# Reciprocal roots of the first graph stage once a group of eight row sets on VectorE, and GpSimd's fill behind every eight sends

## The reference

```
x = x + gnn0(layernorm(x))     # spectral graph layer: U^T, W1, relu, W2, U
x = x + ffn0(layernorm(x))     # 8 experts, best 2 of each token, silu
x = x + gnn1(layernorm(x))     # graph convolution with two batch norms
x = x + ffn1(layernorm(x))     # 8 experts, best 2, and one shared, gelu
layernorm(x) = (x - mean) / sqrt(var + 1e-5)
```

## Time and profile before

| quantity | value |
|---|---|
| median of 3 runs | 1314.97 us |
| the profiled execution | 1320.74 us, span 1318.9 us |
| busy: PE, DVE, ACT, POOL | 84%, 68%, 45%, 37% of the span |
| first stage with its sends | about 289 to 418 us |
| experts of layer 0 | from 422.5 us |
| second graph stage with its sends | about 842 to 1004 us |
| indirect sends of rows, both layers (L1052) | 128, mean 996 ns |

### The profile page before, as it was taken

The page is one execution under the profiler, slowest core; times in us unless marked ns, Lnnn a source line. Parts: engine busy times, 40 slices in busy tenths (PEclk is TensorE's granted clock), DMA queues, the critical chain, the costliest instruction groups (busy, mean ns, idle before and its releaser), DMA issues.

```text
span 1318.9 us, 25232 instructions
## 1 busy us (share of the span) xinstructions
PE 1105.5 (84%) x7060; PEld 924.3 (70%) x7060; DVE 896.8 (68%) x3848; ACT 594.3 (45%) x1786; POOL 488.8 (37%) x539
## 2 busy tenths in 40 slices
PE   3556555658874999999999999798889999999995
PEld 3555544646652888978889754376667998899994
DVE  5777689865775666756667597688753667556683
ACT  2556844507771222212222267466534444444452
POOL 2200000002665444434444461005763555445551
PEclk9999999959996999999999999899889999999998
DMA  9999996000223444323332250001224444233317
GB/s 190 404 428 428 429 426 262 1 0 26 86 87 120 128 123 126 101 72 103 94 91 70 84 207 1 16 5 66 90 85 123 143 144 125 68 114 109 110 55 198
DMA packets 78875, 182.67 MB, mean 138 GB/s; under 512 B 11752, under 2 KB 51699, under 8 KB 75408
## 3 DMA queue, kind: packets, MB, share of 16 engines
q0 software_dynamic: 20544, 112.80, 21.5%
q1 hardware_dynamic: 58192, 68.27, 19.2%
HBM read 65.10 MB, written 119.08 MB: 140 GB/s over the span
## 4 chain that ended last, share of the span: by engine, by line
PE 63%; DVE 25%; issue 5%; ACT 3%; DMA 1%; SPq 1%; another core or an unknown queue 0%; POOL 0%; DVEq 0%; POOLq 0%; ACTq 0%
PE bank L1707 18%; PE bank L1693 17%; PE bank L1696 7%; PE bank L199 4%; PE bank L1933 3%; PE bank L1926 3%; PE bank L1679 2%; PE bank L1860 2%; DVE work L337 2%; DVE u L334 2%; PE bank L900 1%; DVE bnh L1761 1%; PE bank L1441 1%; DVE u L184 1%; DVE u L175 1%
## 5 line engine op out<-in xcount | busy, mean ns | idle before, releaser
L1693 PE MATMUL bank<-work,wide 128*128 128x256 f32 (+3 forms) x994 | 215.4, 330 | 3.3 <-issue 1.9
L1707 PE MATMUL bank<-wide,work 128*128 128x128 f32 x1512 | 216.5, 278 | 0.6 <-DVE work L1623 0.4
L1707 PEld LDWEIGHTS bank<-wide,work 128*128 128x128 f32 x1512 | 198.1, 191 | 9.5 <-DVE work L1623 3.4
L1052 POOL DMA_INDIRECT rows<-tokens,slot x128 | 127.4, 996 | 202.9 <-issue 142.1
L1651 ACT ACTIVATE work<-bank 128x256 f32<-128x256 f32 (+1 forms) x216 | 82.8, 383 | 261.2 <-PE bank L1696 232.8
L1693 PEld LDWEIGHTS bank<-work,wide 128*128 128x128 f32 (+1 forms) x994 | 154.1, 186 | 16.2 <-issue 4.1
L1538 POOL DMA_INDIRECT rows<-wide x100 | 104.7, 1047 | 121.3 <-DVE wide L1575 101.2
L199 PE MATMUL bank<-u 63*64 63x2 f32 (+61 forms) x496 | 73.7, 255 | 66.3 <-DVE u L184 65.3
L1623 DVE TENSOR_TENSOR work<-work,bank 128x256 f32<-128x256 f32 (+1 forms) x216 | 88.3, 417 | 41.1 <-ACT work L1651 36.2
L1559 DVE COPY wide<-wreg 128x1066 f32 (+1 forms) x142 | 100.4, 707 | 21.6 <-issue 18.0
L199 PEld LDWEIGHTS bank<-u 63*64 63x64 f32 (+61 forms) x496 | 64.4, 217 | 71.8 <-DVE u L184 70.5
(11 more groups left out here) (449 smaller groups left out, 2405.0 us busy)
## 6 DMA issues: line engine op xcount, KB each, us to landing
rows<-wide POOLq DMA_DIRECT2D x20, 3432.0 KB, 109.7
wide<-rows SPq DMA_DIRECT2D x100, 260.0 KB
wide<-rows SPq DMA_DIRECT2D x88, 130.0 KB
wreg<-in_w SPq DMA_DIRECT2D x1, 4264.0 KB, 38.8
wreg<-in_w SPq DMA_DIRECT2D x1, 4112.0 KB, 14.1
tokens<-in_x SPq DMA_DIRECT2D x2, 2048.0 KB, 20.2
tokens<-in_xt SPq DMA_DIRECT2D x1, 4096.0 KB, 41.7
tokens<-plane SPq DMA_DIRECT2D x16, 256.0 KB, 5.2
```

The source lines that it names most:

```text
L1052: return self.nc.gpsimd.indirect_dma_start(out=xs, out_offset=bass.IndirectOffsetOnAxis(ap=self.t["slot"][:, q:q + 1], axis=0), in_=self.t ...
L1693: ins = T.matmul(ps[c][0:n, to], w[:, a:a + n], x[:, to], start=True, stop=True)
L1707: ins = T.matmul(ps[4 + j % 2][:, h * P:(h + 1) * P], t["hh"][c][0:n, h * P:(h + 1) * P], w[0:n, at + c * P:at + (c + 1) * P], start=(c == ...
```

## The change

Three edits. `TOGETHER` is 8 instead of 4, so that each fill stands behind eight sends. In `gnn0` the epsilon, ACT's square root, the reciprocal and the offset of each tile are gone; in their place stands `roots(g)` at the end of every even step from step 2, which runs the eleven operations of `inverse_root` and one offset operation for a whole group of eight sets on DVE. And ACT writes the normalised rows of a group's two tiles at the head and at the end of its odd step.

```diff
-TOGETHER = 4
+TOGETHER = 8
 def gnn0_act(nc, act, S, t, ps, route):
+    def normalised(i):
+        act.wait_ge(S("a0_norm"), i // GT + 1)
+        for q in range(PAIRS):
+            at = (i % GT) * PAIRS + q
+            ins = A.activation(t["pay"][:, i * PAIRS + q, 0:P], t["X"][:, i * PAIRS + q, :], ACT.Identity,
+                               bias=t["off"][:, at:at + 1], scale=t["rs"][:, at:at + 1])
+        ins.then_inc(S("a0_xh2"), 1)
-        if 0 <= s - 2 < TILES:
-            i = s - 2
-            act.wait_ge(S("a0_norm"), i + 1)
...
-            ins.then_inc(S("a0_xh2"), 1)
+        if due(s, GT + 1):
+            normalised(s - 3)
...
-        if 0 <= s - 1 < TILES:
-            act.wait_ge(S("a0_var"), s)
-            A.activation(t["sd"][:, 1, :], t["sd"][:, 0, :], ACT.Sqrt).then_inc(S("a0_root"), 1)
+        if due(s, GT + 1):
+            normalised(s - 2)
 def gnn0_dve(nc, dve, own, S, t, ps, route):
-        def variance():
...
-            V.tensor_scalar(t["sd"][:, 0, :], t["mv"][:, :, 1], EPS, None, ALU.add).then_inc(S("a0_var"), 1)
+        def roots(g):
+            dve.wait_ge(S("a0_moments"), GQ * (g + 1))
+            if g:
+                dve.wait_ge(S("a0_xh2"), GT * g)
+            for k in range(ROOT_OPS):
+                inverse_root(V, dve, pair, S("a0_inv"), g, k)
+            dve.wait_ge(S("a0_inv"), (g + 1) * ROOT_OPS)
+            V.scalar_tensor_tensor(out=t["off"], in0=pair["mv"][:, :, 0], scalar=-1.0, in1=t["rs"], op0=ALU.mult,
+                                   op1=ALU.mult).then_inc(S("a0_norm"), 1)
+            dve.wait_ge(S("a0_norm"), g + 1)
-        if old:
-            dve.wait_ge(S("a0_root"), T + 1)
-            if T >= 2:
-                dve.wait_ge(S("a0_xh2"), T - 1)
-            own.chain(V.reciprocal(t["rs"][:, half], t["sd"][:, 1, :]))
-            V.scalar_tensor_tensor(out=t["off"][:, half], in0=t["mv"][:, :, 0], scalar=-1.0, in1=t["rs"][:, half],
-                                   op0=ALU.mult, op1=ALU.mult).then_inc(S("a0_norm"), 1)
-            dve.wait_ge(S("a0_norm"), T + 1)
...
-            variance()
+            for g in due(s, GT):
+                roots(g)
```

More of the change, by code:

```diff
@@ L1341, in gnn0_act @@
             A.copy(t["gm"][i % 2], ps[2][:, :]).then_inc(S("a0_gm"), 1)
-        if 0 <= s - 1 < TILES:
-            act.wait_ge(S("a0_var"), s)
-            A.activation(t["sd"][:, 1, :], t["sd"][:, 0, :], ACT.Sqrt).then_inc(S("a0_root"), 1)
+        if due(s, GT + 1):
+            normalised(s - 2)
 def gnn0_dve(nc, dve, own, S, t, ps, route):
-    V, X = nc.vector, t["X"]
+    V, X, pair = nc.vector, t["X"], t["pair"]
     for s in range(A0_STEPS):
-        T, T1 = s - 2, s - 1
-        old, new = 0 <= T < TILES, 0 <= T1 < TILES
+        T1 = s - 1
+        new = 0 <= T1 < TILES
         xt = X[:, T1 * PAIRS:(T1 + 1) * PAIRS, :] if new else None
@@ L1364, in stats @@
                 dve.wait_ge(S("a0_xadd"), T1 + 1)
+                if T1:
+                    dve.wait_ge(S("a0_moments"), T1 * PAIRS)
             V.bn_stats(t["bn"][:, q, :], xt[:, q, :]).then_inc(S("a0_stats"), 1)
@@ L1370, in moments @@
             dve.wait_ge(S("a0_stats"), T1 * PAIRS + q + 1)
-            V.bn_aggr(t["mv"][:, q, :], t["bn"][:, q, :]).then_inc(S("a0_moments"), 1)
-        def variance():
-            if not new:
-                return
-            dve.wait_ge(S("a0_moments"), (T1 + 1) * PAIRS)
-            V.tensor_scalar(t["sd"][:, 0, :], t["mv"][:, :, 1], EPS, None, ALU.add).then_inc(S("a0_var"), 1)
+            V.bn_aggr(pair["mv"][:, (T1 % GT) * PAIRS + q, :], t["bn"][:, q, :]).then_inc(S("a0_moments"), 1)
+        def roots(g):
[8 more added lines that the diff above has]
+            dve.wait_ge(S("a0_norm"), g + 1)
         def by_choice(k):
@@ L1385, in by_choice @@
                 moments(k - 6)
-            elif k == 10:
-                variance()
-        if old:
-            half = slice((T % 2) * PAIRS, (T % 2 + 1) * PAIRS)
-            dve.wait_ge(S("a0_root"), T + 1)
-            if T >= 2:
-                dve.wait_ge(S("a0_xh2"), T - 1)
-            own.chain(V.reciprocal(t["rs"][:, half], t["sd"][:, 1, :]))
-            V.scalar_tensor_tensor(out=t["off"][:, half], in0=t["mv"][:, :, 0], scalar=-1.0, in1=t["rs"][:, half],
-                                   op0=ALU.mult, op1=ALU.mult).then_inc(S("a0_norm"), 1)
-            dve.wait_ge(S("a0_norm"), T + 1)
         if due(s, GT + 1):
@@ L2194, in build @@
         t["sdi"] = t["sd"][:, :, :].bitcast(I32)
-        t["rs"], t["off"] = sb("rs", [P, 2 * PAIRS])[:, :], sb("off", [P, 2 * PAIRS])[:, :]
+        pair = dict(mv=sb("pair_mv", [P, GQ, 2]), sd=sb("pair_sd", [P, 3, GQ]))
+        pair["sdi"] = pair["sd"][:, :, :].bitcast(I32)
+        t["pair"], t["rs"], t["off"] = pair, pair["sd"][:, 1, :], sb("off", [P, GQ])[:, :]
         nm = sb("norm", [P, 2, 2, PAIRS])
```

## The result

The changed kernel takes 1302.99 us, the median of four runs (1302.79 to 1303.84), against 1315.08 of the kernel before (four runs, 1312.74 to 1316.63). The ratio is 0.9911, 95% interval 0.9894 to 0.9928: faster by 12.1 us. The forecast was 7.6 us, and the time lies 0.5 us under the lower end of the range. The profiled execution took 1302.85 us, its span is 1301.0.

A forecast was written before the change was run, and what follows sets the result against it. The start of layer 0's experts was taken as set by POOL's last send, fed by DVE's loop. Loop 5.5, first steps 1.2 and fill 0.9 made 7.6 us, from 1314.97 to 1307.4 us; range 1303.5 to 1312.5.

The forecast's parts named there:

- The loop: First stage's loop on DVE: period falls from 12.71 to 11.8 us (11.2 to 12.5), six periods giving 5.5 us.
- PE's count: First stage's loop: DVE's wait for PE's count of a group comes out, 0.5 us, between 0 and 1.30.
- The first steps: Layer 0, ahead of the first send: roots of four tiles go, two chains come in; 1.2 us gain, between 0 and 3.0.
- The fill in layer 0: POOL in the first stage: one fill less from group 6 to group 7 counts in full, 0.9 us.
- The sum at the last send: POOL's last send in layer 0 comes 7.6 us earlier: 5.5 + 1.2 + 0.9.
- The products, the load of the first rows and the experts then shift as a block: Layer 0 after POOL's last send: all 7.6 us pass on to the experts.
- 8 x 0.94 = 7.5 us less of POOL is worth 0 here: Layer 1: halving the fills gains nothing, as POOL ends 9 us before PE starts the experts.
- up to 7.5: Layer 1: what fewer fills would be worth in us if the 9 us of cover were gone.
- Locks: Rival: the twelve DVE operations each lose 0.25 us beside POOL's sends; period 14.8, time 1328 us; chance 0.05.
- the upper end that the prediction gave these two: DVE's chain: two tensor_scalar operations held beside POOL each lose 0 to 0.25 us, 0.5 at most; 0.1 taken.
- The second stage moves: Rival: DVE's operations meet other sends there; one more wait for a count gives 1310.8 us, one less 1304.0; chance 0.13.
- The sign by which I would be wrong: Experts of layer 1 starting at another distance from those of layer 0 than 581.45 us.

The follow-up runs named there:

- the fourth: The changed kernel with the fill behind every four sends in layer 1 alone, layer 0 as changed: 1306.85 us, ratio 0.9940.
- the 1310.5: A profiled execution of the kernel before, unchanged, run again for a second trace: 1310.5 us; the median of its eight runs was 1315.21.
- the 1320.74: The first profiled execution of the kernel before, unchanged, whose trace the prediction read: 1320.74 us.

## Why the prediction was wrong

**The loop: right.** Period 11.76 against 11.8; chain 2.45 against 2.36, 0.20 an operation; PE's count 0.54 a group against 0.5. Six periods gave 5.7 us, 5.5 forecast.

**The first steps: right, somewhat low.** The profiled pair shows 0.8. The six profiles without the new roots start their first send at 319.8 us in the mean (318.7 to 320.3), the eight with them at 318.0 (317.2 to 318.7): 1.8, where I had 1.2 between 0 and 3.0.

**The fill in layer 0: right.** From group 6 to group 7 11.51 against 12.27, 0.8 (forecast 0.9), and the kernel with roots alone shows the pace of 12.2 that the prediction gave for the fills as before (12.1). The sum at the last send was 7.2 in the pair, 7.6 forecast; between the means of the four profiles of before and of the four with both edits in layer 0 and six warming products (the changed kernel, the fourth, the fourth with two products more, and the one without layer 1's fills) it is 7.9.

**"The products, the load of the first rows and the experts then shift as a block": failed.** The load came 7.1 us earlier (SP's first at 412.74, before 419.88), the experts 5.9; between the same means the last send is 7.9 earlier and the experts are 7.1. I had carried over 6.93 us for the warming products, a duration taken while the clock was rising. They begin when POOL's small fill is there, and PE's wait for it had shrunk from 3.79 to 0.28 us, where I had 1.0, as PE's limits came 3.7 us earlier and not 5. So, by the estimates above, about 5.9 us of the products ran at 0.50 in place of 3.1. The price was 1.3 us in the pair, 0.8 between the means; four products instead of six gave about as much back.

**"8 x 0.94 = 7.5 us less of POOL is worth 0 here": failed, and this is what put the time out of the range.** It was 3.8 us on top of the rest; with these the 1302.99 would be 1306.8, inside the range. Two things were wrong in the reading of the earlier trace rows. The cover was counted from POOL's last fill, 994.92, to the experts, 1003.93. But the experts need the rows, and these came 5.56 us after the last send had started in the 1310.5: 993.49 + 5.56 = 999.05, against 1003.21 for PE's last product. The cover was about 4.2 us, not 9. And that execution was late in just this stage, 161.89 us against 154.35 to 157.01 in the three others: PE came late and hid POOL. Of this lateness the waits for the counts, among them, are 2.5 us (13.0, against 10.4 to 10.5 in the three others); the rest is not traced to one place. In the other executions of before the two paths arrive within 2 us of each other, and whoever is late decides; in the 1310.5 PE waits 1.89 us, and the clock is at 0.50 in the 5 us behind it. The prediction did say what the cover's loss would cost, "up to 7.5", and gave it no chance.

The sums. The chances add up to 0.78 for faster and 0.17 for same by the terms given, where the prediction has 0.77 and 0.18. In the earlier trace rows the L1174 of 948.84 begins 0.07 us ahead of the send, so it is not inside it; the operations behind it are.

The rivals. Locks did not come in the changed kernel. Grouped by line, the chain's operations in its first stage (times, busy us, mean ns):

```profile
L1174 DVE TENSOR_TENSOR pair_sd<-pair_sd 128x8 f32<-128x8 f32 x24 | 4.4, 183 | 0.8
L1176 DVE TENSOR_TENSOR pair_sd<-pair_sd 128x8 f32<-128x8 f32 x24 | 4.0, 166 | 0.8
L1178 DVE SCALAR_TENSOR_TENSOR pair_sd<-pair_sd 128x8 f32<-128x8 f32 x24 | 4.0, 166 | 0.8
...
L1172 DVE TENSOR_SCALAR pair_sd<-pair_sd 128x8 int32<-128x8 int32 x8 | 1.4, 172 | 0.3
L1170 DVE TENSOR_SCALAR pair_sd<-pair_mv 128x8 f32<-128x8 f32 x8 | 1.4, 171 | 0.3
```

The ten with two inputs run for the most part beside sends and take 166 ns each, but for the first L1174 of six chains, up to 235 ns, where a send starts 0.03 or 0.04 us behind it. By the rule of the Trainium skill, "SBUF — State Buffer", section "Who interferes with whom", the operations with two SBUF inputs would contend with a GpSimd instruction that reads SBUF; so far as a send is such a read, which no run here shows, this trace disagrees. The two scalar operations, L1170 and L1172, have no send beside them at all here: POOL is waiting for the gates that DVE made just ahead of the chain. With roots alone POOL has no such wait, and there they are held (shortest, median and longest in ns; then one chain and POOL beside it):

```profile
L1170 DVE TENSOR_SCALAR pair_sd<-pair_mv x8: 171/468/518, 300.3 to 389.2; 128x8 f32<-128x8 f32 x8
```

```profile
340.13 0.47 DVE L1170 TENSOR_SCALAR pair_sd<-pair_mv 128x8 f32<-128x8 f32 x1
340.63 0.44 DVE L1172 TENSOR_SCALAR pair_sd<-pair_sd 128x8 int32<-128x8 int32 x1
```

```profile
339.62 0.98 POOL L1052 DMA_INDIRECT rows<-tokens,slot  x1 [0.30 <-issue]
340.59 0.45 POOL L1047 MEMSET idle<- 128x400 f32 x1
```

L1170 ends with the send and L1172 with the fill, and the chain takes 2.95 us, 0.5 more, the upper end that the prediction gave these two. So this lock exists, and the change escaped it because both edits came together. "The second stage moves" was the nearest to what happened, as it forecast one wait less and 1304.0, but its mechanism, DVE's operations meeting other sends, was not the one. The sign by which I would be wrong, another distance than 581.45 us between the layers' experts, came: 572.73. But it was a poor sign, as the unchanged kernel shows 572.76, 577.85 and 576.12 in its three other traces.

## What to carry to other kernels

A cover that is read in one execution is worth no more than that execution: before an engine's work is costed at nothing, follow what it releases through the transfer to the instruction that needs it, and ask whether the covering engine was late there by a wait that need not come again. A distance read in one execution cannot be the sign of a change before it is known how far it moves without one. Two edits that each relieve one of two nearly equal paces should be costed together, since either alone may give half or nothing. And where TensorE waits at a seam, the price of the wait is the wait and the low clock behind it; a few products in the wait can be worth more than the wait itself, and too many become the path.

## What the runs showed of the hardware

- The clock behind a wait. With PE's idle time ahead of layer 1's experts at 0.72 (nine profiles), 0.97 and 0.47 us the clock stays at 1.00; at 1.89, 2.34 and 2.43 us it is 0.50 over the first 5 us of the experts. The eight products of L1693 take 1.97 us in the one case and 3.75 in the other. One profile of the first kind is as long as those of the second, the 1320.74, with its 314.97 us: its clock is 1.00, and PE is busy 38.21 of the 40 us from 1083.93 on, 39.64 at the same place of the changed kernel. Why is open.
- Layer 0's six warming products took 6.86 to 7.56 us in the seven profiles where PE had waited 1.7 to 3.8 us for POOL ahead of them, and 7.72 to 8.33 in the four where it had waited 0.2 to 0.3.
- A tensor_scalar operation of 128x8 on DVE beside GpSimd: in the kernel with roots alone L1170 took 468 ns in the median and L1172 430, against 171 and 172 with nothing on GpSimd beside them; the one shown ended with a send, the other with a fill. Operations with two inputs of the same size took 166 ns in the median there, sends beside them or not.
- Rows sent by indirect DMA were back in SBUF for PE 5.5 to 6.0 us after the last send had started on POOL, where PE waited for them (409.55 to 415.06, 988.72 to 994.28, 993.62 to 999.62, and six more).
